# Attention on one core: two subtractions of VectorE placed ahead of the maxima of their steps

## The reference, cut to what matters

```python
x = x + _L0_attn_ref(_layernorm(x, axis=-1), ...)
# in _L0_attn_ref: 16 heads of 8 features
qkv = sn_dense(batch, W_qkv, u_qkv, sigma_qkv)
q, k, v = jnp.split(qkv, 3, axis=-1)
att = jnp.einsum('bhqd,bhkd->bhqk', q, k) * hd ** (-0.5)
att = jnp.where(causal[None, None] == 0, big_neg, att)
att = jax.nn.softmax(att, axis=-1)
x = jnp.einsum('bhqk,bhkd->bhqd', att, v)
x = sn_dense(x, W_proj, u_proj, sigma_proj)
```

## Time and profile before

| | |
|---|---|
| median of 3 runs | 1015.39 us (1014.93 to 1016.19) |
| profiled execution | 1012.83 us |
| its span, first to last instruction | 1011.1 us |
| mean granted TensorE clock | 0.955 of full speed |
| busy over the span | TensorE 876.8 us (87%), VectorE 748.7 (74%), GpSimd 691.8 (68%), ScalarE 599.8 (59%) |
| attention stage | begins at about 270 us of the span |

### The profile page before, as it was taken

One profiled execution on the slowest core, in us unless ns is written; L12 is line 12 of the kernel. 1 busy time (PEld: TensorE's weight loads), 2 busy tenths in 40 slices (PEclk: granted clock), 3 DMA queues, 4 the chain that ended last, 5 costly groups with the idle time before them and its releaser, 6 DMA issues. The chain is left out here.

```text
span 1011.1 us, 26251 instructions
## 1 busy us (share of the span) xinstructions
PE 876.8 (87%) x8024; PEld 664.9 (66%) x8057; DVE 748.7 (74%) x2500; ACT 599.8 (59%) x1575; POOL 691.8 (68%) x1245
## 2 busy tenths in 40 slices
PE   5936599999557999999999999999999974899995
PEld 5833499999524566565656566666666542899995
DVE  8879756555247789998998989898989854655552
ACT  2537466666314666666766666666666661666662
POOL 7709578753123678888888888888887774266664
PEclk9999889999858999999999999999999995899998
DMA  7450032222145553545464445455444301222220
GB/s 213 129 186 0 9 74 68 73 70 63 43 93 111 108 107 93 125 95 120 93 118 96 117 99 110 105 106 108 102 109 95 72 18 49 65 74 67 68 65 22
DMA packets 127017, 89.50 MB, mean 89 GB/s; under 512 B 14187, under 2 KB 117536, under 8 KB 126880
## 3 DMA queue, kind: packets, MB, share of 16 engines
q1 hardware_dynamic: 102752, 52.55, 22.9%
q10 hardware_dynamic: 15488, 17.74, 7.8%
q0 software_dynamic: 8640, 17.53, 6.7%
HBM read 52.09 MB, written 35.34 MB: 86 GB/s over the span
## 5 line engine op out<-in xcount | busy, mean ns | idle before, releaser
L1360 ACT ACTIVATE at_pt<-at_pm 128x512 f32<-128x512 f32 x384 | 228.0, 598 | 118.2 <-PE at_pm L1448 89.9
L1678 DVE TENSOR_REDUCE at_mx<-at_pp 128x2 f32<-128x512 f32 (+1 forms) x384 | 259.7, 679 | 43.0 <-PE at_pp L1437 35.7
L1276 POOL TENSOR_SCALAR_AFFINE_SELECT at_pt<-at_pt 128x256 f32<-128x256 f32 (+1 forms) x384 | 188.0, 493 | 57.1 <-ACT at_pt L1360 54.3
L936 ACT ACTIVATE e_ht<-e_ps_h,b1t 128x128 f32<-128x128 f32 x568 | 161.7, 370 | 84.2 <-PE e_ps_h L981 84.1
L981 PE MATMUL e_ps_h<-e_xnt,e_w1own 128*128 128x128 f32 x1136 | 153.3, 280 | 2.0 <-ACT e_xnt L930 1.3
L992 PE MATMUL e_ps_y<-w,e_ht 128*128 x1136 | 149.1, 275 | 0.0
L981 PEld LDWEIGHTS e_ps_h<-e_xnt,e_w1own 128*128 128x128 f32 x1136 | 141.0, 196 | 3.2 <-ACT e_xnt L930 2.0
L992 PEld LDWEIGHTS e_ps_y<-w,e_ht 128*128 128x128 f32 x1136 | 137.8, 192 | 0.0
L900 POOL DMA_INDIRECT out_dram<-e_y,e_x x71 | 82.3, 1159 | 68.1 <-DVE e_y L1062 51.9
L1062 DVE SCALAR_TENSOR_TENSOR e_y<-e_ps_y,e_x 128x256 f32<-128x256 f32 x72 | 30.3, 421 | 110.3 <-PE e_ps_y L992 110.3
L1469 PE MATMUL at_po<-at_pt,vp 128*32 128x256 f32 (+1 forms) x2048 | 109.8, 332 | 1.6 <-POOL at_pt L1276 1.6
(11 more groups left out here) (324 smaller groups left out, 1744.5 us busy)
## 6 DMA issues: line engine op xcount, KB each, us to landing
at_qkd<-at_part SPq DMA_DIRECT2D x64, 192.0 KB, 3.0
kb<-at_qkd SPq DMA_DIRECT2D x64, 96.0 KB
qs<-at_qkd ACTq DMA_DIRECT2D x64, 96.0 KB
e_x<-buckets SPq DMA_DIRECT2D x71, 66.0 KB, 1.9
x<-e_y SPq DMA_DIRECT2D x35, 128.0 KB, 1.8
rows<-ts_x ACTq DMA_DIRECT2D x16, 264.0 KB, 3.0
ts_x<-in_x_dram SPq DMA_DIRECT2D x16, 256.0 KB, 3.3
x_by_token<-at_xa SPq DMA_DIRECT2D x32, 128.0 KB
```

Source lines behind the costliest of these rows:

```text
L936: last = a.activation(hid_t[j % NB][:, f, :], ps_h[j % NB][:, f, :], ACT.Gelu, bias=c.b1t[:, ds(e, 1), f])
L1276: g.affine_select(out=tile, in_=tile, compare_op=ALU.is_ge, fill=0.0, base=0, pattern=[[0, n], [1, P]], channel_multiplier=-1).then_inc(ma ...
L1360: a.activation(pt[u % RING][:, :], pm[u % 2], ACT.Exp, scale=SCALE).then_inc(exped, 1)
L1678: v.tensor_reduce(out, src, axis=AX.X, op=ALU.max).then_inc(maxed, 1)
```

## The change

In steps 3 and 5 VectorE's program did the maximum of the step first and the subtraction behind it (L1697 in step 3; L1711 in step 5, there behind the reciprocal and the product `on` too). Now each subtraction, with its waits, stands ahead of the maximum of its step, in all turns that have it. Nothing else changes.

```diff
--- before.py
+++ after.py
@@ -1664,6 +1664,17 @@
                         route_a(b - 2, k % 2, u)
                     if has(-3):
                         place_a(b - 3, (k - 3) % 2, u)
+                    if u == 3 and has(3):
+                        h = (k + 1) % 2
+                        wait(dve, a_done, b + 4)
+                        wait(dve, part_done, b + 2)
+                        v.tensor_tensor(rest[h][:, :].rearrange("p (a n) -> p a n", a=2), mi[0].rearrange("p (a n) -> p a n", a=2), part[h][:, 0:6:5, :],
+                                        ALU.subtract).then_inc(r_done, 1)
+                    if u == 5 and has(3):
+                        q = (k + 1) % 2
+                        wait(dve, b_done, b + 4)
+                        v.tensor_tensor(part[q][:, 2:4, :], rest[q][:, :].rearrange("p (a n) -> p a n", a=2), part[q][:, 1:5:3, :],
+                                        ALU.subtract).then_inc(part_done, 1)
                     for o, w in QUERY_TILES[u]:
                         if has(o):
                             n, q = b + o, (k + o) % 2
@@ -1690,12 +1701,6 @@
                         wait(dve, rstd2, b - 1)
                         wait(dve, x2t_tr, (b - 3) * TPB)
                         normalise(xn2[k % 2], x2[(k - 2) % NQ], xn2_done)
-                    if u == 3 and has(3):
-                        h = (k + 1) % 2
-                        wait(dve, a_done, b + 4)
-                        wait(dve, part_done, b + 2)
-                        v.tensor_tensor(rest[h][:, :].rearrange("p (a n) -> p a n", a=2), mi[0].rearrange("p (a n) -> p a n", a=2), part[h][:, 0:6:5, :],
-                                        ALU.subtract).then_inc(r_done, 1)
                     if u == 5 and has(-1):
                         q = (k - 1) % 2
                         wait(dve, otr, b)
@@ -1705,11 +1710,6 @@
                         v.tensor_tensor(on[q][:, :, :].rearrange("p j (h d) -> p (j h) d", d=HD), rows[:, :, 0:HD],
                                         rden[q][:, :, :].rearrange("p j h -> p (j h)").unsqueeze(2).to_broadcast([P, TPB * H, HD]),
                                         ALU.mult).then_inc(on_done, 1)
-                    if u == 5 and has(3):
-                        q = (k + 1) % 2
-                        wait(dve, b_done, b + 4)
-                        v.tensor_tensor(part[q][:, 2:4, :], rest[q][:, :].rearrange("p (a n) -> p a n", a=2), part[q][:, 1:5:3, :],
-                                        ALU.subtract).then_inc(part_done, 1)
                     if u == 6 and has(4):
                         wait(dve, xa_in[k % 2], xa_count(b + 4)(k))
                         spread(xa[k % 2], bn[k % 2], bnd1)
```

## The result

The changed kernel takes 1012.48 us (median of 20 runs, 1010.02 to 1017.72) against 1015.38 us (20 runs, 1013.09 to 1017.54): ratio 0.9979, interval 0.9970 to 0.9988, so 1.2 to 3.0 us faster by the interval, and 2.9 by the medians. Forecast were 1.6 us, with 1013.8 as the likeliest time, 1013.1 to 1014.6 as the forecast's own range and 1012.2 to 1016.4 as the range of 80%. The measured median lies in the range of 80%, near its lower end, and outside the forecast's own.

What follows compares the result with a forecast made beforehand. TensorE (busy 95.8 of 100 us) and VectorE (91.1) can each hold up the middle turns; middle 0, fill -2.1 + 0.5 = -1.6 us, so 1015.39 - 1.6 = 1013.8 us, own range 1013.1 to 1014.6, 80% range 1012.2 to 1016.4.

Steps and rivals of the forecast that it cites:

- The middle turns cost nothing: Turns b=2 to 28: the later maxima of steps 3, 5 and 6 still reach TensorE in time; no cost.
- the spare time: Middle turns, step 3: its later maximum frees the weight load of step 5 with 0.13 us to spare.
- the rival that sat there: Maximum of step 3 late for step 5's load in every middle turn; at 0.15 us a turn 1017.8 us; 8%.
- Turn b=-2, third piece 1.99 us earlier and load of b=-1 2 us earlier: Pipeline fill: L1711 for batch 1 starts 1.99 us earlier, so TensorE's load comes at 306.3 instead of 308.32.
- The maximum of step 6 in b=-1: Fill, VectorE: it starts 1.8 to 2.1 us earlier than 310.18; 2.1 was taken.
- Turn b=0, 0.5 us given back, sum -1.6: Fill: step 3's maximum, now behind L1697, delays TensorE's load by 0.5 us; -2.1 + 0.5 = -1.6 us.
- the fill gains more: Rival, 20%: clock dip goes and turns 1 and 2 lose part of their kb waits; -2.1 to -3.2, about 1012.8 us.
- The dip: Granted clock at 0.51 from 309.90 to 316.80 us, after TensorE stood; it may go, adding up to some 0.4 us.
- L1711 waits out a mask: Rival, 5%: step 5's subtraction waits a whole GpSimd mask (0.49 us) in middle turns; 1018.7 us, deciding from 0.31 us.

Runs made afterwards that it cites:

- e4: Kernel before, with both subtractions ahead of their maxima only from turn b=3 on; ratio 1.0000 to the kernel before.
- e6: Changed kernel plus one added VectorE reduction between subtraction and maximum of step 3, turns b=3 to 28; ratio 1.0036 to the kernel before.
- e5: Kernel before, with only the step 5 subtraction L1711 ahead of its maximum, in turn b=-2 alone; ratio 0.9980 to the kernel before.
- e8: Changed kernel with ScalarE's copy of turned rows for turn b=-2 ahead of its qs DMAs in b=-3; ratio 0.9965 to the kernel before.

## Why the prediction was right

*The middle turns cost nothing:* right within 1.8 us, and right in its steps. The load of step 5 stands where it did, VectorE waits 0.31 us for L1380 (0.3 expected), the maximum of step 6 is 0.08 later (0.12 expected), the consumers of steps 7 and 8 are in time. e4 bears it out in time. What the prediction overlooked is the wait for the DMA of the maxima, which grew. And the spare time was smaller than worked out, 0.07 us instead of 0.13 (e6); the rival that sat there was nearer than the sum had it.

*Turn b=-2, third piece 1.99 us earlier and load of b=-1 2 us earlier:* from the start of the stage, 24.02 against 26.03 us for the piece, 36.62 against 38.37 for the load. Right, with 1.75 for 2.0. The maximum of step 6 in b=-1, counted the same way, was forecast 2.1 earlier; the timeline merges it with that of step 5 into one row (from 307.85, 1.45 us, x2), so it starts at 307.85 + 1.45 - 0.69 = 308.61: 38.16 from the start of the stage against 40.23, 2.07 earlier.

*Turn b=0, 0.5 us given back, sum -1.6:* this is the term that was mis-sized. The load of b=0 is 2.24 us earlier, not 1.6, and from there the gain grows, 2.90 in b=1 and 3.08 in b=3, where I let the later turns only follow. The give-back exists, and in its size: the load of b=0 starts just when the maximum behind the subtraction lets it, 319.54 - 318.10 = 1.44 us behind the end of the copy L1371, where it stood 321.28 - 320.41 = 0.87 behind it, so 0.57 is lost where 0.5 was forecast. Too small is what it is taken from: that copy ends 47.65 us into the stage instead of 50.46, 2.81 earlier, and the sum had 2.1. What I left out is that the third piece no longer lags 1.26 us behind the load in b=-1 and b=0, so each turn sends its pieces earlier still. The rival "the fill gains more" (20%) had this, and its 2.1 to 3.2 us hold the traces' 3.1 and the medians' 2.9: the range held by its rival, not by the forecast. That rival had also named the clock. The dip did go, and in all nine traces with an early third piece in b=-2 and b=-1 the stretch from 40 to 47 us of the stage is at 1.00, while three of the four with a late third piece there have 0.51 to 0.79. But it was worth little: e4, the fourth, has the order of before in the fill and no dip, and still its load of b=3 at 97.34; from b=-1 to b=0 it takes 13.26 us, against 12.96 with the dip.

```profile
309.90:316.80 6.90, 4.37 (x23) 1.44 (x21) 6.00 (x15) 1.88 (x3) 0.72 (x1) 1.00 0.65 139
```

*L1711 waits out a mask:* never for a whole one; the rule behind it shows nevertheless. GpSimd's L1330 has a median of 243 ns in the changed kernel and 562 before, and its L1311, which the third piece now runs across, 600 ns against 198. There GpSimd's operation started second and is the one that gets longer, and L1676 keeps 693 ns (median). The other way round exists too: in three of its 32 turns a pair of masks starts with L1676 or up to 0.03 us ahead of it, and then L1676 takes 0.92 to 0.94 us:

```profile
646.16 1.44 POOL L1276 TENSOR_SCALAR_AFFINE_SELECT at_pt<-at_pt 128x256 f32<-128x256 f32 x2
646.19 0.92 DVE L1676 TENSOR_TENSOR at_part<-at_rest,at_part 128x512 bf16<-128x512 f32 x1 [0.56 <-ACT at_part L1380]
```

That is 0.24 us more, below the 0.31 from which the rival was to decide. This agrees with the Trainium skill ("SBUF — State Buffer", section on the two separate sides), by which a VectorE operation with two SBUF inputs and a GpSimd operation that reads SBUF exclude each other. Whether VectorE then waits for a mask from end to end these rows don't show: 0.24 us is less than the mask's median of 0.42. The longer L1311 costs nothing here: the trace lists nobody that waits for it.

*What stays open:* how much of the 3.1 us each single turn gives (the times are level, and e5's time and trace disagree), why the DMA of the maxima is waited for more often, and what bounds a middle turn.

## What to carry to other kernels

In a software pipeline an instruction may stand behind one whose input comes from the loop that it feeds itself. In the full pipeline that cost nothing that could be seen here, and no list of waits named it; in the first turns, which run through the loop at its latency, it cost its lag in each turn. So look at an order of work twice, in a middle turn and in the first turns, and follow the loop through all turns of the fill, not only the first. And measure a small cover by putting a known delay in front of it and behind it: what looked like 0.13 us was 0.07. And judge a gain of a few us by positions inside the stage in several traces: here one trace scattered by some half a us in the fill and by 1 us and more in the middle.

## What the runs showed of the hardware

A weight load that waited for a maximum started 0.05 us behind its end in one place and 0.12 us in others (507.82 to 507.94 in e6, 319.03 to 319.15 in e8), and such a wait of a load can be listed as "issue" or under a DMA that landed about the same time. The order of before, run with the same work in the fill, had the granted clock at 0.51 (the lower level) for 309.90 to 316.80 us in one execution and at 1.00 (the higher) in another (e4), though TensorE's load had stood for kb about as long just ahead of it, 3.39 and 3.08 us.
